# Expert products of a mixture-of-experts block: from two fp32 products to three fp32r passes over split weights

## The reference, cut to what matters

```python
topk_indices, topk_weights = _router(x, router_weight, e_bias)      # 2 of 16 experts for each token
combine = zeros((T, N_EXPERTS)).at[arange(T)[:, None], topk_indices].add(topk_weights)
h1 = einsum('th,ehi->tei', x, w_up)          # w_up:   16 experts, 512 x 256
a = relu2(h1) * combine[:, :, None]          # relu2(v) = relu(v) * relu(v)
routed = einsum('tei,eih->th', a, w_down)    # w_down: 16 experts, 256 x 512
shared = relu2(hidden_states @ shared_up) @ shared_down
```

## Time and profile before

| | us |
|---|---|
| median of 3 runs | 2444.23 |
| lowest and highest of the 3 | 2442.47, 2448.04 |
| the profiled execution, span | 2451.0 |
| setup and attention, about | 0 to 1500 |
| shared network and router, about | 1500 to 1970 |
| expert phase: tables and zero rows | 1973 to 2005 |
| expert phase: rounds | 2005 to 2335 |
| combine phase | 2338 to 2451 |

### The profile page before, as it was taken

How to read it: one execution, slowest core, us unless ns; L and a number is a source line. 1 busy time by engine, 2 the same in 40 slices (tenths; PEclk the granted TensorE clock), 3 DMA queues, 4 the chain that set the end, 5 groups by cost and what they waited for, 6 DMA issues and landing times. The chain is left out here.

```text
span 2451.0 us, 34688 instructions
## 1 busy us (share of the span) xinstructions
PE 2043.9 (83%) x10812; PEld 1248.9 (51%) x10813; DVE 1115.6 (46%) x2207; ACT 763.2 (31%) x1215; POOL 510.1 (21%) x491
## 2 busy tenths in 40 slices
PE   4899997899987889987998995899999939999900
PEld 1644543654444545434544532676776726666600
DVE  3434553354444345443444435555665323333358
ACT  1244452344452244452244442122221102222200
POOL 0200005100006000006000014444555421000064
PEclk8899998899998899998899997999999969999955
DMA  6212213211213221213222114222222168333388
GB/s 215 52 27 52 44 44 105 52 38 41 52 35 105 52 52 37 42 35 104 52 52 52 32 41 182 71 93 82 90 90 95 65 231 282 127 127 128 116 280 320
DMA packets 104965, 232.49 MB, mean 95 GB/s; under 512 B 20440, under 2 KB 20440, under 8 KB 104812
## 3 DMA queue, kind: packets, MB, share of 16 engines
q1 hardware_dynamic: 81008, 171.86, 24.4%
q0 software_dynamic: 14848, 50.34, 5.7%
q10 hardware_dynamic: 8960, 8.41, 1.2%
HBM read 113.06 MB, written 67.17 MB: 74 GB/s over the span
## 5 line engine op out<-in xcount | busy, mean ns | idle before, releaser
L459 DVE TENSOR_REDUCE mx<-ring 128x1 f32<-128x512 f32 (+3 forms) x640 | 369.4, 632 | 395.6 <-PE ring L569 305.0
L367 ACT ACTIVATE pr<-sc 128x1024 f32<-128x1024 f32 (+3 forms) x384 | 307.9, 810 | 416.3 <-PE sc L601 343.2
L617 PE MATMUL O<-pr,V 128*32 128x512 f32 (+3 forms) x3072 | 343.0, 524 | 34.7 <-ACT pr L367 29.5
L598 PE MATMUL sc<-stk 128*128 128x512 f32 (+3 forms) x768 | 271.0, 427 | 42.4 <-ACT stk L356 42.4
L598 PEld LDWEIGHTS sc<-stk 128*128 128x128 f32 x768 | 144.2, 200 | 292.2 <-issue 189.4
L322 POOL TENSOR_TENSOR oT<-oV,oD 128x512 f32<-128x512 f32 x32 | 41.0, 1282 | 1165.8 <-DVE oD L481 1165.8
L569 PE MATMUL ring<-stk 96*128 96x512 f32 (+3 forms) x768 | 258.7, 434 | 27.4 <-DMA stk<-st 26.9
L569 PEld LDWEIGHTS ring<-stk 96*128 96x128 f32 x768 | 154.8, 215 | 38.8 <-issue 16.4
L1475 PE MATMUL ue<-wu_e,xT_e 128*128 x632 | 151.2, 383 | 0.1
L1489 PE MATMUL de<-wd_e,aT_e 128*128 x316 | 148.5, 593 | 0.0
L481 DVE RECIPROCAL oD<-oD 128x512 f32<-128x512 f32 x32 | 105.5, 3330 | 88.5 <-ACT oD L379 88.5
(11 more groups left out here) (233 smaller groups left out, 3478.3 us busy)
## 6 DMA issues: line engine op xcount, KB each, us to landing
stk<-st SPq DMA_DIRECT2D x192, 256.0 KB, 5.0
x_e<-xs SPq DMA_DIRECT2D x79, 256.0 KB, 2.6
ys<-y_e SPq DMA_DIRECT2D x79, 256.0 KB, 2.0
oT<-in_L_attn_x_dram ACTq DMA_DIRECT2D x16, 512.0 KB, 5.7
xr<-in_L_attn_x_dram SPq DMA_DIRECT2D x32, 256.0 KB, 2.8
x1d<-h SPq DMA_DIRECT2D x32, 256.0 KB, 2.0
xb<-x1d SPq DMA_DIRECT2D x32, 256.0 KB, 3.1
part<-y_sh SPq DMA_DIRECT2D x32, 256.0 KB, 2.0
```

The costliest lines, as they stand in the source:

```text
L367: nc.scalar.activation(pr[:, g % 3, :, off:], sc[g % 2][:, :, off:], ACT.Exp, scale=SCALE).then_inc(exp_done, 1)
L459: nc.vector.tensor_reduce(mx[:, heads[0]:heads[-1] + 1, qt, part], bank[:, 0:len(heads) * w].rearrange("p (e k) -> p e k", e=len(heads)), ...
L598: last = nc.tensor.matmul(sc[g % 2][:, e, off:], K.stk[:, p % 2, 1, e, i * P:(i + 1) * P], K.stk[:, p % 2, 0, e, c * CH + off:(c + 1) * CH ...
L617: last = nc.tensor.matmul(O[row:row + 32, off:], V[:, col:col + DH], pr[:, g % 3, e, off:], start=(i == 0), stop=(i == 4 * c + 3))
```

## The change

Both expert products are done in three fp32r passes. A value is the sum of a high part (the value rounded to fp32r) and a low part (the rest). The product is high by high, high by low and low by high; an fp32r product goes through the array once, a float32 product is two records per product before.

- POOL loads an expert's raw weights into a ring of three (`raw_e`), casts them to the high part and subtracts to the low part (`split`), 2 casts and 2 subtractions of 128x1024 each. The split weights go to a ring of eight experts (`wup_e`, `wdn_e`). From expert 8 on, a split waits until the last tile of the expert eight places before has left PE (`d_done`, against the table `endi`). The load of expert e+3 is issued behind the split of expert e. The wait of the weight loads for the zero rows is gone.
- The up product: for each of 4 blocks one pass of `xhi` over 512 columns (high and low weights side by side) and one of `xlo` over 256 columns. The halves are added afterwards: ACT copies the right half (`cross_e`), DVE adds (`h1_e`), and one DVE instruction makes relu2 of it (`a_e`), where ACT's relu and DVE's square stood.
- The down product: 6 passes of 512 columns.
- ACT now makes `xhi`, `cross_e`, `ahi` and `y_e`; DVE makes `xlo`, `h1_e`, `a_e`, `alo`.
- A third table, `eslot`, gives the tile's place in the ring; it has a few more DVE instructions and a third transpose. Dummy tiles take expert 15 in place of expert 0.
- The setup phase clears and frees its semaphores at its end and adds a barrier.

```diff
-        sem = lambda n: ctx.enter_context(nc.semaphore(n))
+        held = []
+        def sem(n):
+            held.append(nc.alloc_semaphore(n))
+            return held[-1]
...
+    nc.clear_and_free_semaphores(held)
+    nc.all_engine_barrier()
...
+            def split(e):
+                z, w = e % RAW, e % WR
...
+                pool.wait_ge(raw_in[z], (e // RAW + 1) * 32)
+                if e >= WR:
+                    done = pool.value_load(endi[0:1, e - WR:e - WR + 1], min_val=1, max_val=NET + 1)
+                    pool.wait_ge(d_done, done)
+                    apart(pool)
+                nc.gpsimd.tensor_copy(up[:, :, 0, :], up_raw).then_inc(whi_ready, 1)
+                nc.gpsimd.tensor_copy(dn[:, :, 0, :], dn_raw).then_inc(whi_ready, 1)
+                pool.wait_ge(whi_ready, 2 * e + 2)
+                nc.gpsimd.tensor_tensor(up[:, :, 1, :], up_raw, up[:, :, 0, :].bitcast(f32), ALU.subtract).then_inc(w_ready, 1)
+                nc.gpsimd.tensor_tensor(dn[:, :, 1, :], dn_raw, dn[:, :, 0, :].bitcast(f32), ALU.subtract).then_inc(w_ready, 1)
...
         @block.vector
...
                 if has(j + 2 if known(j) else j):
-                    dve.wait_ge(r_ready, j + 3)
+                    dve.wait_ge(cross_ready, j + 3)
+                    wait(dve, a_ready, j + 2)
+                    nc.vector.tensor_tensor(h1[:, :], ub[s % 2][:, 0:EI], cross[:, s % 2, :], ALU.add).then_inc(h1_ready, 1)
+                    dve.wait_ge(h1_ready, j + 3)
                     wait(dve, ta_done, j + 1)
-                    nc.vector.tensor_tensor(a[:, s % 2, :], r[:, s % 2, :], r[:, s % 2, :], ALU.mult).then_inc(a_ready, 1)
+                    nc.vector.scalar_tensor_tensor(a[:, s % 2, :], h1[:, :], 0.0, h1[:, :], ALU.max, ALU.mult).then_inc(a_ready, 1)
...
         @block.tensor
...
-                    e = expert(j + 2)
-                    pe.wait_ge(w_ready, e + 1)
-                    pe.wait_ge(xT_ready, j + 3)
-                    wait(pe, r_ready, j + 1)
+                    e, w = lookup(eid, j + 2), lookup(eslot, j + 2)
+                    pe.wait_ge(w_ready, e * 2 + 2)
+                    pe.wait_ge(xlo_ready, j + 3)
+                    wait(pe, h1_ready, j + 1)
...
+                        at = w * (2 * WX) + k * 2 * EI
+                        both = lambda: nc.tensor.matmul(ub[s % 2][:, :], xhi[:, s % 2, k, :], wup[:, bass.ds(at, 2 * EI)],
+                                                        start=(k == 0), stop=(k == KC - 1), skip_group_check=True)
...
+                    terms = [(a_, h, k) for k in range(EC) for a_, h in ((ahi, 0), (ahi, 1), (alo, 0))]
+                    for n, (a_, h, k) in enumerate(terms):
+                        last = nc.tensor.matmul(db[s % 2][:, :], a_[:, s % 2, k, :], wdn[:, bass.ds(w * (2 * EC * D) + (2 * k + h) * D, D)],
+                                                start=(n == 0), stop=(n == len(terms) - 1))
```

More of the change, by code:

```diff
@@ L1246, in expert_phase @@
         sem = lambda n: ctx.enter_context(nc.semaphore(n))
+        wup = sb("wup_e", [P, WR * KC * 2 * EI], f32r)
+        wdn = sb("wdn_e", [P, WR * EC * 2 * D], f32r)
+        raw = sb("raw_e", [P, RAW, WN])
         x = sb("x_e", [P, XR, D])
-        xT = sb("xT_e", [P, 2, KC, P])
-        r = sb("r_e", [P, 2, EI])
+        xhi, xlo = sb("xhi_e", [P, 2, KC, P], f32r), sb("xlo_e", [P, 2, KC, P], f32r)
+        cross = sb("cross_e", [P, 2, EI])
+        h1 = sb("h1_e", [P, EI])
         a = sb("a_e", [P, 2, EI])
-        aT = sb("aT_e", [P, 2, EC, P])
+        ahi, alo = sb("ahi_e", [P, 2, EC, P], f32r), sb("alo_e", [P, 2, EC, P], f32r)
         y = sb("y_e", [P, XR, D])
@@ L1269, in expert_phase @@
         base = sb("base", [P, E])
-        inside, other, mine_e = sb("inside", [P, E]), sb("other", [P, E]), sb("mine_e", [P, E])
-        rowf = sb("rowf", [P, 4])
+        inside, other = sb("inside", [P, E]), sb("other", [P, E])
+        rowf = sb("rowf", [P, 6])
         padf = sb("padf", [P, E])
@@ L1275, in expert_phase @@
         moved = sb("moved", [P, 2 * NTILE])
-        padi = sb("padi", [P, E], i32)
+        padi, endi = sb("padi", [P, E], i32), sb("endi", [P, E], i32)
+        eid, eslot, xrow = sb("eid", [P, NET], i32), sb("eslot", [P, NET], i32), sb("xrow", [P, NET], i32)
         iotas, zeroed, step, tables = sem("iotas"), sem("rows_zeroed"), sem("table_step"), sem("tables")
         in_columns, in_rows = sem("in_columns"), sem("in_rows")
-        w_in = [sem(f"we_in{i}") for i in range(2)]
-        w_ready, padded = sem("we_ready"), sem("padded")
+        raw_in = [sem(f"raw_e_in{i}") for i in range(RAW)]
+        whi_ready, w_ready, padded = sem("whi_e_ready"), sem("we_ready"), sem("padded")
         block = ctx.enter_context(nc.Block())
@@ L1362, in _ @@
+            for e in range(RAW):
+                fetch(e)
+            for e in range(E):
+                if e == WR:
+                    pool.wait_ge(tables, 1)
+                split(e)
+                if e + RAW < E:
+                    pool.wait_ge(w_ready, 2 * e + 2)
+                    fetch(e + RAW)
         @block.scalar
@@ L1420, in _ @@
             nc.vector.tensor_copy(padi[:, :], padf[:, :])
+            nc.vector.tensor_scalar(endi[:, :], ends[:, :], float(PRIMED), None, ALU.add)
             ts(inside[:, :], starts[:, :], jf[:, 0:1], None, ALU.is_le)
@@ L1452, in _ @@
             pe.wait_ge(in_columns, 1)
-            for n in range(2):
+            for n in range(3):
                 last = nc.tensor.transpose(txb[0][0:1, n, 0:NET], rowf[0:NET, 2 + n:3 + n], K.ident[0:NET, 0:NET])
@@ L1456, in _, with lookup @@
             pe.wait_ge(tables, 1)
-            def expert(t):
-                return pe.value_load(K.eid[0:1, t:t + 1] if known(t) else K.eid[0:1, bass.ds(t, 1)], min_val=0, max_val=E - 1)
+            def lookup(table, t):
+                return pe.value_load(table[0:1, t:t + 1] if known(t) else table[0:1, bass.ds(t, 1)], min_val=0,
+                                     max_val=E - 1 if table is eid else WR - 1)
             def round_(j, s):
@@ L1479, in round_ @@
                     pe.wait_ge(a_ready, j + 2)
-                    wait(pe, aT_ready, j)
+                    wait(pe, alo_ready, j)
                     for k in range(EC):
@@ L1484, in round_ @@
                 if has(j):
-                    e = expert(j)
-                    pe.wait_ge(aT_ready, j + 1)
+                    w = lookup(eslot, j)
+                    pe.wait_ge(alo_ready, j + 1)
                     wait(pe, y_ready, j - 1)
-                    for k in range(EC):
-                        last = nc.tensor.matmul(db[s % 2][:, :], aT[:, s % 2, k, :], K.wd[:, bass.ds(e * (EC * D) + k * D, D)],
-                                                start=(k == 0), stop=(k == EC - 1))
+                    terms = [(a_, h, k) for k in range(EC) for a_, h in ((ahi, 0), (ahi, 1), (alo, 0))]
+                    for n, (a_, h, k) in enumerate(terms):
+                        last = nc.tensor.matmul(db[s % 2][:, :], a_[:, s % 2, k, :], wdn[:, bass.ds(w * (2 * EC * D) + (2 * k + h) * D, D)],
+                                                start=(n == 0), stop=(n == len(terms) - 1))
                     last.then_inc(d_done, 1)
```

106 lines of the change are left out of this document (60 added, 46 removed).

## The result

The changed kernel takes 2454.81 us (median of 14 runs, 2448.98 to 2459.47); the kernel before, run in turn with it, 2444.11 (14 runs, 2436.64 to 2451.68). The ratio is 1.0041, its 95% interval 1.0027 to 1.0055: slower by 0.4%, 10.7 us. The forecast was 2437, 7 us faster; the time lies in its range and on the other side.

A forecast was written before the change was run, and what follows sets the result against it. The array bounded the 4.10 us expert round; after the change PE's sequencer would. Terms -10.8 - 1.5 + 4 + 0.7 - 1 + 1.6 = -7.0 on 2444.2 gave 2437; forecast 2430 to 2444 (chance 0.50), full range 2420 to 2460.

The forecast's parts named there:

- loop rounds: 72 rounds of the expert loop: each falls from 4.10 to 3.95 us, -10.8 us in all, bounds -14 to 0.
- first and last rounds: The 7 expert rounds outside the loop, partly empty: -1.5 us.
- POOL beside DVE: 28 rounds beside POOL's splits: a_e, with two SBUF inputs, held by subtractions, +4 us, bounds 0 and 17.
- tables: Start of the expert phase: about four more dependent table steps of some 0.2 us ahead of the zero rows, +0.7 us.
- rest of the start: First tiles: four weight transfers no longer start beside them, tile 0's longer chain included, -1 us, bounds 0 and -2.5.
- setup: End of setup, before attention's first transfer: one more barrier, +1.6 us, bounds 0.5 and 3.
- The array: PE's matmul work in an expert round: falls from 4.10 to 3.46 us, 3.98 with the upper bound.
- The sequencer becomes the bound: PE's sequencer in each round: work grows 2.95 to 3.95 us, above the array's 3.46; gain 0.15 us, not 0.64.
- rival C: Expert rounds: no change, the 0.15 pause is the sequencer's own; round 4.1 us, total 2448; chance 0.15.
- Weights: Split weights for expert tiles: ready before needed, nothing waits unless an expert costs POOL over 14 us.
- A: Expert rounds: the array stays the bound, round 3.46 to 3.98 us; at 3.46 total 2398; chance 0.12.
- B: Rounds beside POOL: port holds a_e more, slower than before; losses 11 to 41 us, 2454 at half; chance 0.20.

The follow-up runs named there:

- the late fetch: Slot-from-expert kernel, with only expert 0's weights fetched at the start, experts 1 to 3 behind the zero rows, first split behind the tables: 2403.74 us.

## Why the prediction was wrong

By its own steps, all in the changed kernel's profiled execution:

```
term                        forecast (bounds)       measured
loop rounds                 -10.8 (-14 to 0)        +6.0   (72 x 0.083)
first and last rounds        -1.5                    -1.4
POOL beside DVE              +4 (0 to 17)            +1.8
tables                       +0.7                    +2.0
rest of the start            -1 (-2.5 to 0)          +3.2   (+4 in the mean of all kernels)
setup                        +1.6 (0.5 to 3)         +0.6
sum                          -7.0                    +12.2
```

**The array.** Right: 3.46 us was its estimate, and the five kernels with one read less all stand at 3.46. The lower bound of 0.12 for a pass of 256 columns was the right choice. That the sum fits to the hundredth is luck, though: ue and de take 2.96 us instead of 2.81, since the first pass behind transposes is 0.31 apart and not 0.23, and tx and ta take 0.50 instead of 0.65.

**The sequencer becomes the bound.** Right, and shown from both sides: PE idle on "issue" in front of ue, no wait in the sequencer's steps, 0.64 us a round for a read more, 0.72 for a read less (long reads included), and for the loss of eight of fourteen matmuls nothing beyond the two addresses and the long reads that went with them. The price of a read (0.65) was right too. The sum of the steps, 3.95, is right in part by luck: it was read from a single round, so it lacks the loop's end (0.12 a round in the mean), and without that the shortest steps come to 3.84.

**The size of the round.** This is the step that failed, and it decided the sign. A margin of 0.15 us, 72 times, was the whole gain, and it stood on a read of 0.30 us that was taken to be constant. All 100 reads in the middle of before's phase were that; but the trace of before has none at 0.6 to 1.2 us behind a store, and the longer sequence moved one into that place: +0.14 us a round. The other 0.09 is the small spread of some 27 steps, for which nothing was counted. The pause of 0.15 that the prediction took for a full queue was one: it is gone where the array isn't full. So the round was not 3.95 but 4.18, even above rival C's 4.1, and the loop's rounds brought +6.0 us in place of -10.8. The bound of 0 for this term was no bound at all: nothing excluded a loss, once the sequencer's 3.95 to 4.1 stood against 4.10.

**POOL beside DVE.** The mechanism is right: a_e took up to 2.64 us beside a subtraction, and all of that goes when its inputs are not both in SBUF. Casts of 1.04 us and subtractions of 2.34 were as forecast. It was sized too high for this kernel: five of the loop's first nine rounds lost 0.2 to 0.6 us each in halts for a_e, 1.7 together, and no later one did, since a_e is ready 1.6 us ahead of the sequencer's wait for it rather than the 1.3 that the prediction had left. With the round at 3.46 and the splits later the same port costs 5.6 us. The prediction looked for two SBUF inputs among the new DVE instructions alone. One that it didn't count, the 128x1 `rowf` at 1973.46 above, stood in the kernel before as well, and took 1.01 us beside a cast. Rows of POOL and DVE in the changed kernel's first rounds:

```profile
2012.78 2.53 POOL L1392 TENSOR_TENSOR wdn_e<-raw_e,wdn_e 128x1024 fp32r<-128x1024 f32 x1
...
2014.07 1.53 DVE L1442 SCALAR_TENSOR_TENSOR a_e<-h_e 128x256 f32<-128x256 f32 x1
```

The small table instruction at 1975.76, 16 elements with one input, took 2.14 us and ended with POOL's subtraction. The Trainium skill, page SBUF — State Buffer, section Who interferes with whom, says just that: tensor_scalar between SBUF operands can take the shared pair and wait for it. This one came behind the last table and delayed nothing. What did lie on the way to `tables` is the `rowf` of 1.01 us (0.16 without the cast) and a tensor_scalar of 0.52 (before 0.23). The prediction had named held table instructions and left them out of its sum; they were worth 1.1 us of the 2.0, the added instructions the rest.

**The start.** The second step that failed, 4 us off with its sign. The prediction counted as a gain that four transfers of weights no longer start beside the first tiles, and didn't ask what starts in their place: three experts at once and a fourth and fifth behind them, 5 MB beside the zero rows. The DMA engines' share was 0.92 there instead of 0.64:

```profile
1977.00:1997.00 20.00, 0.00 (x0) 0.00 (x0) 12.44 (x7) 0.00 (x0) 19.23 (x14) 0.50 0.92 299
```

```profile
1981.00:1998.00 17.00, 0.00 (x0) 0.00 (x0) 3.41 (x5) 0.00 (x0) 0.00 (x0) 0.50 0.64 243
```

SyncE's reads grew from 0.27 to 0.46 us in the middle and 0.87 at most, and rows and tiles landed later.

**Setup.** +0.6, at the lower bound. **Weights.** Right: PE's waits name a split once in the phase, for 0.3 us at 2161.7, and the sequencer doesn't halt there, so no split was late.

**The rivals.** A was the array's round of 3.46 and 2398, given 0.12: wrong for this kernel; the one with a read less has that round, and takes 2403. B had the right sign and the wrong cause. C came nearest in mechanism. What was missing is a rival for the sequencer itself: its margin of 0.15 turned into a loss.

## What to carry to other kernels

Count the sequencer of the busiest engine as a resource of its own, read by read and address by address, before array work is exchanged for table reads; a value that one register step can compute from one already there (e & 7) is worth 50 us here against a second table. When the forecast gain is a small difference of two nearly equal sums, its bounds must reach to the other side. A transfer that no longer starts somewhere starts somewhere else: look at what it now lies beside, and at who reads tables there.

## What the runs showed of the hardware

- A sequencer's read of a table in SBUF takes 0.30 us on PE and 0.27 on SyncE. On PE it mostly takes 0.4 to 0.6 if it begins 0.6 to 1.2 us behind the issue of a 256 KB store (over 0.40 in 181 of 225 such reads, in 13 of 1393 others, over the eleven changed kernels), and on SyncE up to 0.87 at a DMA share of 0.92.
- A read more per round costs 0.64 us on a bound sequencer, a read less gave 0.72 (long reads included), and on a sequencer with 1 us to spare a read costs nothing.
- Moving work that shares a port out from beside one phase brings it beside the next: with the slot computed from the expert, the late fetch won 7 us at the start and lost 5 in the rounds, until the instruction that shared the port took an operand from PSUM.
